# Cross attention of a gated transformer block: probabilities with keys on partitions, maxima subtracted in PSUM, value product in 32-column tiles

## The reference, cut to what matters

```python
def xattn(q, k, v, q_norm_w, k_norm_w, w_out):     # q: (4, 256, 256); k = v: (4, 256, 64)
    q = rms_norm(q, q_norm_w); k = rms_norm(k, k_norm_w)
    # 16 query heads of 16, 4 key/value heads of 16: four query heads share one key head
    q, k = rope(q), rope(k)
    scores = einsum('bgnqd,bgkd->bgnqk', qg, k) / 4
    scores = where(causal, scores, -1e30)
    attn = softmax(scores)
    out = einsum('bgnqk,bgkd->bgnqd', attn, v)
    return out @ w_out.T
x = x + tanh(g_xattn) * xattn(layernorm(x), ctx, ctx, ...)
x = x + tanh(g_ffn) * ffn(layernorm(x), ...)       # self-attention, then experts
```

## Time and profile before

| | |
|---|---|
| median of three runs | 551.22 us (550.22 to 552.91) |
| span of the profiled execution, first to last instruction | 548.8 us |
| outside the span, median less span | 2.4 us |
| mean granted TensorE clock | 0.974 of full speed |

### The profile page before, as it was taken

One profiled execution on the slowest core, in us unless ns is written; L12 is line 12 of the kernel. 1 busy time (PEld: TensorE's weight loads), 2 busy tenths in 40 slices (PEclk: granted clock), 3 DMA queues, 4 the chain that ended last, 5 costly groups with the idle time before them and its releaser, 6 DMA issues.

```text
span 548.8 us, 11087 instructions
## 1 busy us (share of the span) xinstructions
PE 470.7 (86%) x3380; PEld 424.1 (77%) x3380; DVE 446.4 (81%) x1215; ACT 306.9 (56%) x821; POOL 319.2 (58%) x362
## 2 busy tenths in 40 slices
PE   0379999989867999999989999889989997679996
PEld 0269998889755788888879889878879796569896
DVE  5857677876489999989989999989989999963644
ACT  2148777676325666656656567557556565463341
POOL 7952707801245958949848768758767663151352
PEclk9999999999978999999998999999989999997899
DMA  8000000220112342243333242252242330000011
GB/s 288 2 2 2 1 2 2 78 78 2 39 39 59 76 114 67 55 133 76 76 96 76 66 131 69 59 134 57 65 126 57 76 77 2 1 2 0 1 40 38
DMA packets 17962, 32.46 MB, mean 59 GB/s; under 512 B 3972, under 2 KB 6152, under 8 KB 17800
## 3 DMA queue, kind: packets, MB, share of 16 engines
q1 hardware_dynamic: 14008, 23.35, 16.0%
q10 hardware_dynamic: 3920, 8.69, 5.7%
HBM read 14.20 MB, written 1.05 MB: 28 GB/s over the span
## 4 chain that ended last, share of the span: by engine, by line
DVE 31%; PE 27%; issue 22%; POOL 9%; ACT 6%; DMA 3%; DVEq 1%; ACTq 1%; POOLq 0%; SPq 0%
PE bank L1220 9%; DVE room L875 6%; PE bank L1173 5%; POOL split_room L245 4%; PE bank L1156 3%; DVE room L869 3%; DVE PR L995 3%; DVE o_parts L939 3%; DVE sm L950 2%; POOL qk_room L423 2%; DVE V L881 2%; DVE yacc L986 2%; ACT PR L519 2%; DMA qk_room<-qk_room 2%; DVE PR L994 1%
## 5 line engine op out<-in xcount | busy, mean ns | idle before, releaser
L423 POOL TENSOR_TENSOR qk_room<-qk_room,cst_sb 128x512 f32<-128x512 f32 x64 | 88.5, 1383 | 49.9 <-DMA qk_room<-qk_room 49.9
L570 ACT ACTIVATE PR<-sm,nm 128x128 f32<-128x128 f32 (+1 forms) x128 | 57.3, 448 | 93.7 <-DVE nm L950 93.7
L245 POOL TENSOR_TENSOR split_room<-room,split_room 128x256 fp32r<-128x256 f32 (+1 forms) x60 | 72.0, 1201 | 19.6 <-ACT split_room L550 19.6
L1220 PE MATMUL bank<-hH,qk_parts 128*128 128x512 f32 x256 | 83.2, 407 | 0.0
L875 DVE TENSOR_TENSOR room<-room,qk_room 128x512 f32<-128x512 f32 x64 | 67.2, 1050 | 10.8 <-POOL qk_room L423 10.8
L869 DVE TENSOR_TENSOR room<-qk_room,cst_sb 128x512 f32<-128x512 f32 x64 | 58.6, 916 | 0.0
L1220 PEld LDWEIGHTS bank<-hH,qk_parts 128*128 128x128 f32 x256 | 50.4, 197 | 9.2
L544 ACT ACTIVATE qk_room<-bank,qk_bias 128x512 f32<-128x512 f32 x64 | 43.5, 680 | 22.0 <-DVE room L875 21.5
L1220 PE MATMUL bank<-hL,qk_parts 128*128 128x512 f32 x128 | 53.0, 414 | 3.0 <-issue 1.8
L519 ACT ACTIVATE PR<-bank,nxm 128x128 f32<-128x128 f32 (+1 forms) x128 | 45.8, 434 | 16.1 <-DVE nxm L837 11.9
L1173 PE MATMUL bank<-PTs,room 128*128 128x128 f32 x384 | 50.7, 275 | 0.1
(11 more groups left out here) (201 smaller groups left out, 1398.1 us busy)
## 6 DMA issues: line engine op xcount, KB each, us to landing
qk_room<-qk_room SPq DMA_DIRECT2D x128, 128.0 KB, 2.4
stg<-in_wqkv ACTq DMA_DIRECT2D x6, 768.0 KB, 5.5
stge<-in_we ACTq DMA_DIRECT2D x7, 256.0 KB, 3.1
stg<-in_wqkv SPq DMA_DIRECT2D x2, 768.0 KB, 6.3
stgo<-in_wo ACTq DMA_DIRECT2D x6, 256.0 KB, 3.0
x_sb<-in_x SPq DMA_DIRECT2D x4, 256.0 KB, 6.2
bv_sb<-in_bv SPq DMA_DIRECT2D x1, 1024.0 KB, 4.8
out_y<-yacc SPq DMA_DIRECT2D x4, 256.0 KB, 2.1
```

Of the source, the lines that this page charges most:

```text
L245: eng.tensor_tensor(low, v, high.bitcast(F32), ALU.subtract).then_inc(s["split_low"], 1)
L423: pool.tensor_tensor(v, v, cst_sb[:, col:col + 256].unsqueeze(1).to_broadcast([P, 2, 256]), ALU.mult).then_inc(s["chunk_sw"], 1)
L570: ins = act.activation(PR[:, q, a:e], sm[:, q, a:e], ACT.Exp, bias=nm[:, q, t:t + 1], scale=-1.0, accum_out=rs[:, q, t:t + 1])
L1220: ins = pe.matmul(outp, l, r, start=(m == 0), stop=(m == n - 1))
```

## The change

Scores, masks and maxima stay as they are. The exponentials no longer come from the bank with queries on partitions. Instead TensorE makes the scores a second time, transposed (`x_turned`): the key block is the weights and the queries of four heads are the moving operand, 512 columns; on a diagonal block a matmul of 512 columns adds the transposed mask; and four matmuls of 128 columns add the negated maxima, whose weights are a column of `nxm` (now bf16) repeated 128 times. One `Exp` of 512 columns then gives the probabilities with keys on partitions. `x_turn` and both `pt_copy` are gone. Pieces of this second pass are blocks (key block, query block) = (0,0), (0,1), (1,1) for z = 0, 1, 2. In `x_values` each head's matmul has 32 columns of weights (VP = 32) and writes 32 partitions of `bank[4]`.

The lags become TLAG = 3 for `x_turned` and VLAG = 5 for `x_values`; `x_scores` now waits for the maxima of piece p - 2; the side work moves by some pieces. `residual(b)` begins four pieces later, and for batch 2 runs in pieces 46 to 51. `norm_turn(2)` stands behind the loop.

```diff
-VP, VZ = 128, 96
+VP = 32
+TLAG, VLAG = 3, 5
...
-        nxm = sb("nxm", [P, 2, 4])
+        nxm = sb("nxm", [P, 3, 8], BF16)
...
             def q_evac(b, X, t):
                 n = m6["Q", b, X, t]
                 act.wait_ge(s["m6_pe"], n + 1)
+                if b:
+                    act.wait_ge(s["st_pe"], XP * (b - 1) + 6 * (X + 1))
...
+            def x_exp(p):
+
+                act.wait_ge(s["st_pe"], p + 1)
+                if p >= 4:
+                    act.wait_ge(s["pv_pe"], p - 3)
+                act.activation(probs[:, p % 4, :], PT_B[p % 2][:, :], ACT.Exp).then_inc(s["s_exp"], 1)
...
-                for n, h in enumerate(heads):
-                    ins = act.activation(PR[:, p % 2, n * width:(n + 1) * width], S_B[p % 2][:, n * width:(n + 1) * width],
-                                         ACT.Exp, bias=nxm[:, p % 2, n:n + 1])
...
-                if p >= 2 and not copied_by_act(p - 2):
-                    pt_copy(dve, p - 2)
...
-                if k >= 6 and b:
-                    residual(b - 1, k - 6)
...
+                b1, phase = divmod(p - XP - 10, XP)
+                if b1 >= 0 and phase < 6:
+                    residual(b1, phase)
...
                 if p >= 2:
-                    pe.wait_ge(s["s_exp"], p - 1)
+                    pe.wait_ge(s["s_max"], p - 1)
...
-            def x_turn(p):
+            def x_turned(p):
+
+                b, k = divmod(p, XP)
+                m, z = divmod(p, 3)
+                g, h = k // 3, 4 * (k // 3)
+                kt, t = block_of(z)
+                pe.wait_ge(s["s_max"], 3 * m + (1 if z == 0 else 3))
+                if p >= 2:
+                    pe.wait_ge(s["s_exp"], p - 1)
+                by_head = PT_B[p % 2][:, :].rearrange("p (h n) -> p h n", h=4)
+                pe.matmul(by_head, kT[:, b, g, kt * P:(kt + 1) * P], qT[:, h // 8, t, h % 8:h % 8 + 4, :], start=True, stop=False)
+                if kt == t:
+                    pe.matmul(by_head, mask_bf, ident_bf.unsqueeze(1).to_broadcast([P, 4, P]), start=False, stop=False)
+                for n in range(4):
+                    ins = pe.matmul(PT_B[p % 2][:, n * P:(n + 1) * P], nxm[:, m % 3, 4 * t + n:4 * t + n + 1].to_broadcast([P, P]), ident_bf,
+                                    start=False, stop=(n == 3))
+                ins.then_inc(s["st_pe"], 1)
+
+            def x_values(p):
...
-                for n in range(4):
-                    ins = pe.transpose(PT_B[p % 2][:, n * P:(n + 1) * P], PR[:, p % 2, n * P:(n + 1) * P], ident)
-                ins.then_inc(s["pt_pe"], 1)
...
-                for n, h in enumerate(heads):
-                    for kt in range(t + 1):
-                        a = VZ + VP * (XG * (2 * b + kt) + g) - 32 * (h % 4)
-                        ins = pe.matmul(bank[4][:, c:c + P], room[:, a:a + P], PTs[:, p % 2, (n * (t + 1) + kt) * P:(n * (t + 1) + kt + 1) * P],
-                                        start=(h % 4 == 0 and kt == 0), stop=(h % 4 == 3 and kt == t))
+                for n in range(4):
+                    ins = pe.matmul(bank[4][32 * n:32 * (n + 1), t * P:(t + 1) * P], v_slots[:, XG * (2 * b + kt) + k // 3, :],
+                                    probs[:, p % 4, n * P:(n + 1) * P], start=(z != 2), stop=(z != 1))
                 ins.then_inc(s["pv_pe"], 1)
...
-            for p in range(NPX + 3):
+            for p in range(NPX + VLAG):
...
+                if TLAG <= p < NPX + TLAG:
+                    x_turned(p - TLAG)
...
+                if p >= VLAG:
+                    x_values(p - VLAG)
+            norm_turn(B - 2)
```

More of the change, by code:

```diff
@@ L505, in oT_evac @@
                 act.activation(oT[:, m % 2, :], bank[4][:, 0:256], ACT.Copy).then_inc(s["oT_ready"], 1)
+            def x_exp(p):
[3 more added lines that the diff above has]
+                act.activation(probs[:, p % 4, :], PT_B[p % 2][:, :], ACT.Exp).then_inc(s["s_exp"], 1)
             q_evac(0, 0, 0)
             q_evac(0, 0, 1)
-            for p in range(NPX):
+            for p in range(NPX + VLAG):
                 b, k = divmod(p, XP)
[L511 to L517, removed]
-                for n, h in enumerate(heads):
-                    ins = act.activation(PR[:, p % 2, n * width:(n + 1) * width], S_B[p % 2][:, n * width:(n + 1) * width],
-                                         ACT.Exp, bias=nxm[:, p % 2, n:n + 1])
[L521 to L528, removed]
-                    h_high(b - 2)
[L530 to L535, removed]
+                if p < NPX:
+                    if k in (3, 4):
+                        q_evac(b, 1, k - 3)
+                    if k == 8 and b:
+                        o_evac(b - 1)
+                    if k in (9, 10) and b + 1 < B:
+                        q_evac(b + 1, 0, k - 9)
+                if TLAG <= p < NPX + TLAG:
+                    x_exp(p - TLAG)
+                if k == 7 and b >= 2:
+                    h_high(b - 2)
+                if p >= 7 and p % 3 == 1:
+                    oT_evac((p - 7) // 3)
             h_high(B - 2)
@@ L829, in hidden_t, with x_max @@
                 dve.memset(small[:, 110:111], 0.0).then_inc(s["hT_ready"], 1)
[L831 removed]
+            def x_max(p):
                 b, k = divmod(p, XP)
                 g, t, heads = piece(k)
+                m, z = divmod(p, 3)
+                a = (0, 4, 6)[z]
                 dve.wait_ge(s["s_pe"], p + 1)
[L835 to L837 removed]
+                if z == 0 and m >= 3:
+                    dve.wait_ge(s["st_pe"], 3 * (m - 2))
+                dve.tensor_reduce(nxm[:, m % 3, a:a + len(heads)], S_B[p % 2][:, :].rearrange("p (h n) -> p h n", h=len(heads)),
                                   AX.X, ALU.max, negate=True).then_inc(s["s_max"], 1)
[L839 to L840 removed]
+            for p in range(NPX + VLAG):
+                b, k = divmod(p, XP)
+                if p < NPX:
+                    x_max(p)
                 if p == 0:
@@ L846, in _ @@
                     norm_q(b + 1)
-                if k == 2 and b >= 2:
+                if k == 6 and b >= 2:
                     hidden_t(b - 2)
-                if p >= 6 and p % 3 == 0:
-                    norm_out((p - 6) // 3)
-                if k == 5 and b + 1 < B:
+                if p >= 9 and p % 3 == 0:
+                    norm_out((p - 9) // 3)
+                if k == 6 and b + 1 < B:
                     pack(b + 1, 0)
-                if k >= 6 and b:
-                    residual(b - 1, k - 6)
-                if k == 10 and b + 1 < B:
+                if k == 11 and b + 1 < B:
                     pack(b + 1, 1)
[L857 to L860, removed]
+                b1, phase = divmod(p - XP - 10, XP)
+                if b1 >= 0 and phase < 6:
+                    residual(b1, phase)
             hidden_t(B - 2)
```

62 lines of the change are left out of this document (25 added, 37 removed).

## The result

The changed kernel takes **532.45 us** (median of four runs, 531.03 to 534.88) against 551.34 us for the kernel before on the same chip: a ratio of 0.967, 95% interval 0.962 to 0.972. That is 18.9 us faster. The prediction was 540.4 us, 10.8 us faster, with a range of 529 to 557 us. The time lies in the range and on the forecast side; the gain is 1.7 times the forecast one. The forecast's own narrower range, 534 to 546 us, misses it, and the nearest of the stated times is the 530 us of rival C.

The account below looks back on a forecast made before the run. TensorE's instructions were taken to bound the cross-attention stage. Second pass +7.0, value product -16.3 and waits -1.5 us sum to -10.8 us: 540.4 us against 551.22, range 529 to 557 us.

Parts of the forecast that it names:

- rival C: Value product: all four heads run side by side, 0.22 us a piece, kernel at 530 us; chance 0.14.
- What bounds the stage: Cross-attention stage: lasts as long as TensorE's instructions, priced by distances between starts; TensorE busy 99.45 of 106 us.
- The second pass, 7.0 us more: Transposed scores: 1.76 us per group in place of 1.32 us for transposes, over 16 groups 7.0 us more.
- Rival D: Second score pass: the maxima's weights load slowly, 10.6 us more, 551 us, no change; chance 0.07.
- The value product, 16.3 us less: Value matmuls in column tiles: 0.56 us a piece in place of 0.90, over 48 pieces 16.3 us less.
- The two records of one float32 matmul use the same tile, and must follow each other: Value product: records of one head 0.11 us apart, next head overlapping, so five steps where there were eight.
- The change of tile costs nothing that this trace can show: Value product: entering or leaving 32-column tiles is free, judged from eight expert-weight transposes taking 1.35 us as summed.
- rival B: Value product: the array empties at each change of tile, 0.165 us twice per piece, 15.8 us more, 556.2 us; chance 0.12.
- the prediction's own sign: Value product: last maxima record to first value record takes 0.055 us, or 0.2 or more if the array empties.
- the factor 2.38: Value product: skill page's measured gain for three column tiles of one-record matmuls; gives 0.38 us a piece, some 9 us faster.
- The waits, 1.5 us less: TensorE's waits: 1.1 us less at the start, 1.7 less for turned queries, 1.3 more before norm_turn(2).
- Rival A: Value product: the tiles run one after another, nothing gained there, 556.7 us, slower; chance 0.15.

Follow-up runs that it names:

- experiment 3: Changed kernel, but from piece 12 on all four value matmuls of a piece write the same column tile; 549.4 us, ratio 0.997.
- experiments 4 to 6: Changed kernel with: paired value products, 530.8 us; unaltered, 532.7; residual(2) packed into four pieces, 530.9; that plus pairs, 530.4; a useless ScalarE copy per exponential, 537.2.
- the one with both edits: Changed kernel with residual(2) packed into four pieces and the value products of z = 1 and z = 2 together; 530.4 us, ratio 0.962.
- Experiment 1: Changed kernel with the value product back in the full width (128 columns of weights), second score pass and lags kept; 550.3 us, ratio 1.000.
- Experiment 2: Kernel before with the 32-column value tiles alone, transposes, copies, lags and waits as before; 544.9 us, ratio 0.990.
- experiment 4: Changed kernel with the value products of pieces z = 1 and z = 2 one right behind the other; 530.8 us, ratio 0.965.

## Why the prediction was right, and where it was off

- **What bounds the stage** was right: TensorE, priced by distances between starts. The gain came in the stage (18.5 of 19.2 us of the span).
- **The second pass, 7.0 us more.** Right: five times 0.22 and twelve times 0.055 us per group. The broadcast weights cost no more than others: the twelve records a group are 0.055 us apart. Rival D is out. Where the values run in the full width they start 0.05 us dearer behind bf16 matmuls.
- **The value product, 16.3 us less.** Right in kind, mis-sized: 48 x (0.90 - 0.46) = 21.1 us. Two steps of it failed, in opposite directions. "The two records of one float32 matmul use the same tile, and must follow each other", is right as far as it goes (0.107 us apart in experiment 3), but the step drawn from it, that each head starts one record behind the head before it, is wrong. The first records of all four heads start within 0.02 us, the second ones 0.13 us behind them: two steps where the prediction counted five, 0.21 us of streaming, as in rival C. "The change of tile costs nothing that this trace can show" is wrong for these pieces: it costs 0.24 us a visit, a cost of rival B's kind at three quarters of its price of 0.33 us. By the prediction's own sign, the first value record comes 0.15 us behind the last maxima record, between the forecast 0.055 and rival B's 0.2. Why the eight transposes of the earlier trace rows showed none of it stays open; their first weights, unlike those of the value product, were loaded while a matmul of the full width (begun at 506.30) ran:

```profile
506.30 0.08 PEld L1387 LDWEIGHTS bank<-cst_sb,gate 128*4 128x4 f32 x1
```

So that row need not show the case that it was used for.
- **The rules of the Trainium skill.** Its rule in "TensorEngine Tiling (Array Packing)", Key Properties, that a change of mode drains the engine, pointed the right way, and I had let one row overrule it. The estimate from the factor 2.38 of the Trainium skill's "TensorE: Matmul & The Clock Gate", Part 3, was 0.38 us a piece; measured 0.46, a factor of 1.96. That page has its factor for three tiles and 512 moving columns; here it is four tiles and 128 columns.
- **The waits, 1.5 us less.** Mis-sized: the stage shrank by 18.5 us, of which 14.1 us is work (7.0 - 21.1), so 4.4 us are left for waits and the clock. The scores of piece 2 start at 31.64 us, not at 32.89 (1.1 us forecast). All of the 3.4 us for queries went and not half. The waits for maxima (2.4 us from 30 to 126 us) are as long as those for exponentials were in the same stretch. The waits for `nh` are 3.4 us, 2.0 of them ahead of the first projection where the prediction had 1.3. The prediction has no term for the clock: the distance between bf16 records of 128 columns fell from 0.11 to 0.055 us at 32.8 us and not at 35.6, about 1.4 us (half of the 2.7 us that the kernel before still worked at 1.2 GHz, an estimate). That is luck of the execution: in the kernels of experiments 4 to 6, which have the same code up to there, it fell between 32.6 and 36.7 us, but at 26.3 us in the one with both edits. How the 4.4 us divide is not closed. Both rows of the start:

```profile
31.64 0.37 PE L1137 MATMUL bank<-yacc,qk_room 128*128 128x256 bf16 x1 [0.24 <-DVE nxm L827]
...
32.84 0.22 PE L1137 MATMUL bank<-yacc,qk_room 128*128 128x128 bf16 x1 [0.40 <-DVE nxm L827]
```

- **What the prediction did not see** is how the parts depend on each other. Experiment 1 shows that the second pass and its schedule take away some 8 us of waits when TensorE has its old load. Experiment 2 shows that tiles alone bring 6 to 7 us, since ScalarE then holds TensorE up. Together they bring 19. A sum of TensorE's terms with one line for waits gives the right total only by chance. Which part of the schedule (the longer lags, the release by maxima, the four probability buffers) takes the waits away was not separated, except that ScalarE's load is about 3 us of it.
- **Rival A** is out by experiment 3: it describes that kernel, which took 549.4 us. The prediction gave A and B together 0.26 where its own chances are 0.15 and 0.12.

## What to carry over

The values of a head, 16 columns and one of ones, fill a small part of a weight load of 128 columns. In column tiles of 32 the streaming of four heads takes as long as that of one (by the rule of experiment 4), and a fixed price for entering and leaving comes on top (0.24 us here). More matmuls per visit save that price on TensorE (0.25 us a pair in experiment 4); that they shorten this kernel was not shown. When a change takes work from the engine that bounds a stage, ask in the same breath whether the engines that feed it keep up: half of a good idea brought 1% here and the other half nothing, and both 3.4%.

## What the runs showed of the hardware that I had not expected

- Matmuls in four column tiles start together: of the eight records of four float32 matmuls, four start within 0.02 us and the other four 0.13 us behind them, while eight records in one tile start 0.11 us apart.
- A visit to the 32-column tiling costs 0.10 us ahead of the first record and 0.14 us behind the last, whether it holds 8 or 16 records and whether they use one tile or four.
- A weight load that reads one bf16 column 128 times costs what a plain one costs: 0.055 us from matmul to matmul.
